# Cross-attention of layers 2 to 4 with the probabilities as stationary operand: 32x32 block transposes on VectorE and 32-row products in place of TensorE transposes

## The reference

```python
q = layernorm(x) @ Wq.T + bq             # 64 x 32 tokens, 16 heads of 16 features
k = ctx @ Wk.T + bk                      # 64 x 257 keys
v = ctx @ Wv.T + bv
scores = einsum('bhqd,bhkd->bhqk', q, k) / 4     # + mask or bias
attn = softmax(scores, axis=-1)
out = einsum('bhqk,bhkd->bhqd', attn, v)
x = x + out @ Wo.T + bo
```

## Time and profile before

| what | value |
|---|---|
| median of 3 runs | 3512.74 us |
| the profiled execution's own time, its span | 3512.3 us |
| PE busy in it | 3266.2 us, 93% |
| DVE, ACT, POOL busy | 63%, 41%, 29% |
| l1x, l2x, l3x together | about 1320 us, each about 440 us |
| steady stretch of l1x (14 tiles) | 379 us, PE busy 375.0 |

### The profile page before, as it was taken

One profiled execution on the slowest core, in us unless ns is written; L12 is line 12 of the kernel. 1 busy time (PEld: TensorE's weight loads), 2 busy tenths in 40 slices (PEclk: granted clock), 3 DMA queues, 4 the chain that ended last, 5 costly groups with the idle time before them and its releaser, 6 DMA issues. The chain is left out here.

```text
span 3512.3 us, 105565 instructions
## 1 busy us (share of the span) xinstructions
PE 3266.2 (93%) x39150; PEld 2585.9 (74%) x39150; DVE 2217.2 (63%) x7505; ACT 1454.0 (41%) x4212; POOL 1003.2 (29%) x1620
## 2 busy tenths in 40 slices
PE   7978999999987999999999999888999999988799
PEld 6767887777766888888877777765666777767576
DVE  4767226666667988889556666763334666668455
ACT  2334335555532333333255555541111555556222
POOL 0112113333243444444323333442110111112421
PEclk9989999999997999999999999979999999999699
DMA  6643332222112000000011111042112111110323
GB/s 222 212 177 154 115 100 58 57 57 54 62 40 103 3 2 2 2 2 2 13 44 45 43 43 44 2 146 98 46 46 69 43 39 39 39 35 2 114 79 113
DMA packets 145872, 225.26 MB, mean 64 GB/s; under 512 B 14216, under 2 KB 121480, under 8 KB 143816
## 3 DMA queue, kind: packets, MB, share of 16 engines
q1 hardware_dynamic: 138816, 203.16, 18.4%
q0 software_dynamic: 6816, 18.69, 1.5%
HBM read 201.03 MB, written 38.74 MB: 68 GB/s over the span
## 5 line engine op out<-in xcount | busy, mean ns | idle before, releaser
L3303 POOL TENSOR_TENSOR l1fu_second_weighed<-l1fu_second,l1fu_parts 128x256 bf16<-128x256 bf16 x384 | 273.0, 739 | 342.9 <-DVE l1fu_second L3544 336.0
L3355 PEld LDWEIGHTS l1fu_ps_u<-l1f_xnT_all,l1f_key_in 128*128 128x128 f32 x2048 | 252.5, 195 | 17.4 <-issue 11.2
L3355 PE MATMUL l1fu_ps_u<-l1f_xnT_all,l1f_key_in 128*128 (+1 forms) x2048 | 255.0, 279 | 8.7 <-issue 5.5
L3366 PE MATMUL l1fu_ps_y<-l1f_key_out,l1fu_units 128*128 128x256 f32 x1024 | 250.6, 389 | 1.7 <-DVE l1fu_units L3552 1.7
L3366 PEld LDWEIGHTS l1fu_ps_y<-l1f_key_out,l1fu_units 128*128 128x128 f32 x1024 | 185.7, 190 | 33.3 <-issue 6.0
L3417 ACT COPY l1fu_plane<-l1fu_ps_p 128x512 f32<-128x512 f32 x128 | 75.1, 586 | 249.4 <-PE l1fu_ps_p L3345 249.4
L3539 DVE TENSOR_TENSOR l1fu_first<-l1fu_index,l1fu_counted 128x1024 bf16<-128x1024 bf16 x128 | 165.0, 1289 | 20.3 <-PE l1fu_ps_p L3345 17.6
L3425 ACT ACTIVATE l1fu_units<-l1fu_ps_u 128x512 f32<-128x512 f32 x128 | 76.6, 599 | 150.6 <-PE l1fu_ps_y L3366 138.5
L3011 DVE TENSOR_TENSOR l2f_hidden<-l2f_hidden,l2f_ps_u 128x512 f32<-128x512 f32 x55 | 37.8, 688 | 148.9 <-PE l2f_ps_u L2755 139.1
L1020 ACT ACTIVATE l2x_scores<-l2x_scores,l2x_minus_big 128x257 f32<-128x257 f32 x256 | 129.2, 513 | 2.5 <-DVE l2x_minus_big L1104 2.4
L1020 ACT ACTIVATE l1x_scores<-l1x_scores,l1x_minus_big 128x257 f32<-128x257 f32 x256 | 129.2, 513 | 2.1 <-DVE l1x_minus_big L1104 2.1
(11 more groups left out here) (747 smaller groups left out, 8379.8 us busy)
## 6 DMA issues: line engine op xcount, KB each, us to landing
rows_by_expert<-in_zeros_dram SPq DMA_DIRECT2D x1, 17544.0 KB
l0x_ctxT<-in_ctx_T_dram SPq DMA_DIRECT2D x32, 514.0 KB, 5.2
l0x_ctx_rows<-in_ctx_dram SPq DMA_DIRECT2D x64, 256.0 KB, 3.4
l0f_w<-in_L_ffn_w_dram SPq DMA_DIRECT2D x16, 1024.0 KB, 5.1
l1x_ctx_sb<-in_ctx_T_dram SPq DMA_DIRECT2D x64, 256.0 KB, 2.8
l2x_ctx_sb<-in_ctx_T_dram SPq DMA_DIRECT2D x64, 256.0 KB, 2.8
l3x_ctx_sb<-in_ctx_T_dram SPq DMA_DIRECT2D x64, 256.0 KB, 2.8
l1x_mask_raw<-in_mask_int_dram SPq DMA_DIRECT2D x16, 514.0 KB, 3.9
```

What stands on the lines that cost most here:

```text
L3303: last = nc.gpsimd.tensor_tensor(second_weighed[:, k % 2, part], second[:, k % 2], parts[:, 1 - par, part, TC * k:TC * k + TC].unsqueeze(2 ...
L3355: last = nc.tensor.matmul(ps_u[:, k % 2, j, :], key_in[:, c, JS * k + j, :], xnT_all[:, c, bass.ts(tile, P)], start=(c == 0), stop=(c == C ...
L3366: last = nc.tensor.matmul(ps_y, units[:, k, j, :], key_out[:, JS * k + j, :], start=(k + j == 0), stop=(k == K - 1 and j == JS - 1))
```

## The change

Per batch, in each of the three cross-attentions:

- VectorE turns the probabilities within 32x32 blocks by one transpose of 128x1152 (9 blocks of 32 keys for each of 4 banks, the ninth filled up with zeros) in place of TensorE's 8 transposes, and of the copies out of PSUM on ScalarE and VectorE.
- `values` makes the values in the layout that this needs: 64 products of 128x32 by 64 columns, four beside each other in the array, in place of 4 of 128x128 by 256.
- `outputs` uses the turned probabilities [32 keys, 128] as the stationary operand: 36 products of 32 rows x 128 columns with 68 moving columns, four row groups beside each other, each row group into a bank of its own. The values carry a column of ones, which gives the sum; the last key is a ninth step with one row.
- `turn_shares`, `weigh`, `inverse`, `shares` are gone. ScalarE copies the values and (in four pieces of 32 partitions) the outputs; once per tile VectorE divides (`norm_context`), TensorE turns the tile (`turn_mixed`, two transposes) and ScalarE keeps it with the bias.
- keys and values have PSUM of their own; the outputs lie in the score banks, behind column 260.
- Start: GpSimd fills four tiles with zeros or ones, and four small DMAs spread the last key's values over partitions.

```diff
-            def turn_probs_1(at, before, draining):
-                for r in range(R):
-                    last = nc.tensor.transpose(ps_p[:, r, :], scores[:, b, r, 0:P], ident)
-            def turn_probs_2(at, before, draining):
-                for r in range(R):
-                    last = nc.tensor.transpose((ps_p2 if draining else ps_p)[:, r, :], scores[:, b, r, P:K2], ident)
...
+            def values(at, before, dst=ps_v):
+                for kb in range(KB):
+                    for c in range(C):
+                        for j in range(2 * HH):
+                            last = nc.tensor.matmul(dst[32 * j:32 * j + 32, kb, :], ctx_sb[:, b, c, 32 * kb:32 * kb + 32],
+                                                    by_group(c, j), start=(c == 0), stop=(c == C - 1),
+                                                    skip_group_check=True, tile_position=(0, 32 * j))
...
+            def outputs(at, before, ahead2):
+                if before:
+                    pe.wait_ge(per_batch["o_kept"][before[0]], before[1])
+                if ahead2:
+                    pe.wait_ge(per_batch["biased_ready"][ahead2[0]], ahead2[1])
+                pe.wait_ge(s["tail_values_put"], n)
+                pe.wait_ge(per_batch["v_kept"][b], n)
+                wait(pe, per_batch["probs_turned"][b], n)
+                for kb in range(KB + 1):
+                    for j in range(2 * HH):
+                        keys_of = slice(32 * j, 32 * j + (32 if kb < KB else 1))
+                        values_of = v[keys_of, b, kb] if kb < KB else v_last[keys_of, b]
+                        last = nc.tensor.matmul(ps_o[:, j, :], probsT[keys_of, b % 2, kb].rearrange("p r q -> p (r q)"),
+                                                values_of.rearrange("p r e -> p (r e)"), start=(kb == 0),
+                                                stop=(kb == KB), skip_group_check=True, tile_position=(32 * j, 0))
...
+                nc.vector.transpose(probsT[:, b % 2].rearrange("p k r q -> p r k q"),
+                                    scores[:, b].rearrange("p r (k q) -> p r k q", q=32)).then_inc(per_batch["probs_turned"][b], 1)
...
+            def fill():
+                nc.gpsimd.memset(v_tail[:], 0.0)
+                nc.gpsimd.memset(scores[:, :, :, KEYS:WIDE], 0.0)
```

More of the change, by code:

```diff
@@ L771, in turn @@
-            def turn(i, first, last):
-                n = i + 1
[L773 to L789, removed]
@@ L926, in tile_output, with turn @@
                 last.then_inc(s["y_ready"], 1)
-            def turn(i, first, last):
+            def turn(i, first, last, ahead_norm):
                 n = i + 1
@@ L1041, in turn @@
-            def turn(i, first, last):
+                act.wait_ge(per_batch["o_ready"][b], n)
+                if b == 0:
+                    after(act, s["ctx_normed"], n - 1)
+                for r in range(R):
+                    last = nc.scalar.copy(summed[32 * b:32 * b + 32, :, r],
+                                          ps_o[32 * r:32 * r + 32, :, HE * r:HE * r + HE].rearrange(
+                                              "p (c h) e -> p c h e", c=C))
+                last.then_inc(per_batch["o_kept"][b], 1)
@@ L1042, in turn, with keep_oT @@
+            def keep_oT(n):
+                act.wait_ge(s["mixed_turned"], n)
+                after(act, s["y_ready"], n - 1)
+                kept(oT[:], by_chunk(ps_mixed), "bv").then_inc(s["oT_kept"], 1)
+            def turn(i, first, last, ahead_norm):
                 n = i + 1
                 for t in range(BT):
-                    now, before2, ahead, ahead3 = (batch(t + k, n, first, last) for k in (0, -2, 1, 3))
-                    keep_probs(now, before2)
-                    if not last and t == 2:
+                    now, ahead, ahead3 = (batch(t + k, n, first, last) for k in (0, 1, 3))
+                    if ahead:
+                        exps(ahead, range(0, 2))
+                    if not last and t == 1:
@@ L1176, in turn @@
                     if ahead2:
                         maxima(ahead2)
[L1178 to L1187 removed]
+                    if not first and t == 0:
+                        norm_context(n - 1)
@@ new lines, in turn @@
+                    if not last and t == 1:
+                        spread_q(n + 1)
+                    if ahead_norm and t == 2:
+                        tile_stats(i + 2, n + 2)
+                    if not first and t == 2:
+                        add_output(i - 1, n - 1)
+                    if ahead:
+                        turn_probs(ahead, before)
+                    if ahead_norm and t == 3:
+                        tile_normed(i + 2, n + 2)
+            for i in range(2):
+                tile_stats(i, i + 1)
+                tile_normed(i, i + 1)
```

411 lines of the change are left out of this document (174 added, 237 removed).

## The result

The changed kernel takes 3968.54 us, median of 4 runs (3951.24 to 3981.26); the kernel before 3516.97 on the same chip (3510.6 to 3523.42). The ratio is 1.129, interval 1.1265 to 1.1318: 452 us slower, where 3596 had been predicted.

What follows compares the result with a forecast made beforehand. TensorE's stream was taken to set the pace. 15 steady tiles each at +1.36, +1.36 and +1.86 us gave +69; with ends +9 and starts +6, 3512.3 became 3596 us, range 3515 to 3760.

Steps and rivals of the forecast that it cites:

- sum per tile: TensorE's steady cross-attention tile: -7.76 + 9.20 + 0.22 + 0.20 = +1.86 us in l3x, +1.36 in l1x and l2x.
- Outputs: 36 products per batch in 18 waves of four row groups, 120 ns each and 0.14 first load: 2.30 us.
- Removed work: Both halves of the transposes, the shares and the old outputs go from TensorE: 7.76 us per tile.
- What both kernels do alike: Keys, scores, queries and output projection on TensorE were said to fall out of the difference.
- The new wait: Plain batch's outputs wait in the score banks until VectorE has read the scores of t+2: 0.2 us per tile.
- Hidden work: VectorE's block transpose, at most 1.60 us, and ScalarE's copies, about 0.22 each, stay hidden: about 15 and 18 of 28 us.
- the likeliest case: Whole kernel at 3596 us, its own range 3543 to 3643; chance 0.62.
- Ends: After each cross-attention's last values, 11.8 us to the last product in l2x, and 3 us more each: +9.
- Short loads: Rival: 32-row loads cost a fourth or hide fully, outputs 1.22 us, whole kernel 3402 us; chance 0.13.
- loads that take turns: Rival: one full-width load at a time for all row groups, outputs 8.13 us, whole 4646 us; chance 0.07.
- Waiting loads: Rival: a load waits for the product before it, wave 171 ns, or 162 by l3a's rate; whole 3733 us; chance 0.12.
- A wash: Rival: outputs at 105 ns a wave, no new wait, free ends: 3523 us at most; chance 0.06.

Runs made afterwards that it cites:

- the half columns: Changed kernel with half the values made in the loop; its outputs with 34 of 68 moving columns: 3540.95 us, or with 64 of 128 stationary columns: 3485.42 us.
- the kernel with all the work: Changed kernel, values of key blocks 0 to 2 made twice by an inner loop, blocks 5 to 7 left out: 3692.22 us, ratio 1.052.
- the written-out loop: Changed kernel with only TensorE's loop over tiles 1 to 13 written out in the three cross-attentions: 3736.9 us, ratio 1.065.
- the one at 3485 us: Changed kernel with half the values made in the loop, and key blocks 1 to 7 of the outputs with 64 of 128 stationary columns: 3485.42 us.
- six blocks: Changed kernel with key blocks 6 and 7 of the values left out in the loop's tiles: 3657.89 us.
- the four-tile kernel: Kernel before with TensorE's loop at four tiles per pass, 3 passes and two tiles written out: 3554.58 us, ratio 1.0126.

## Why the prediction was wrong

The direction was right, the size was not. The step that failed is the **sum per tile**: its terms were all prices of work, and "the time from one start to the next" was taken to be their sum. The change part by part counted 176 products becoming 458 only as time on the array. They are also text of a loop, and most or all of that text had to be fetched again in every pass: a term of 309 us that the sum has at nothing. The 442.7 us between the profiles' cross-attentions divide so:

| part | predicted, us | measured, us |
|---|---|---|
| 14 steady tiles x 3 at their prices (28.75 for a tile without stalls) | 64 | 76 |
| stalls and slow clock in the same tiles: 1516.1 - 42 x 28.75 | 0 | 309 |
| starts, first tile, ends | 20 | 58 |

Of the 309 us TensorE stands for 183.5; the other 125 are work at the lower clock behind the stalls.

The terms of work come out near the forecast in sum, and that is luck in part. *Values*: 1.92 predicted, 1.92 to 1.93 measured. *Outputs*: 2.30 predicted, 2.17 measured, 64 records (16 waves) in 1.81 to 1.84 us, 113 to 115 ns a wave instead of 120. The bound by the load was right, as the half columns show. An estimate by the rule of the Trainium skill in "TensorE: Matmul & The Clock Gate", section "LDWEIGHTS (loading the stationary operand)", is 107 ns a wave and 1.93 + 0.14 = 2.07 us, about as far below as the forecast was above. *turn_mixed*: 0.22 predicted, 0.31 measured.

*Removed work* was 7.4 us per tile and not 7.76. The plain batch that was read the earlier trace rows is the dearest of the four; in the others the old outputs take 0.58 or 0.59 instead of 0.70, and behind the queries the first half of the transposes takes 0.44. In the kernel before, and for the next reading two rows of the changed kernel:

```profile
772.76 0.65 PE L913 MATMUL l1x_ps_o<-l1x_probsT,l1x_v 128*32 128x64 f32 x32
773.35 0.66 PE L878 MATMUL l1x_ps_p<-const,l1x_scores 128*128 128x128 f32 x4
...
749.34 1.99 PE L850 MATMUL l1x_ps_k<-l1x_ctx_sb,weights 128*128 128x256 f32 x8
751.17 1.03 PE L917 MATMUL l1x_ps_x<-weights,l1x_oT 128*128 128x256 f32 x4
```

*What both kernels do alike* didn't fall out of the difference. Keys behind scores take 751.17 - 749.34 = 1.83 us, and as much ahead of turn_xn, where they took 1.73 behind the transposes; turn_xn takes 0.31 instead of 0.22, the output projection 0.96 instead of 0.86. The reason wasn't tried. *The new wait* for the maxima: a plain batch has 727.06 - 725.10 = 1.96 us from keys to outputs, 0.23 above 1.73, but 0.10 of that is in all keys that stand behind scores, and the wait is 0.13 where 0.2 was predicted. VectorE's last maximum ends at 726.96, the outputs start at 727.06:

```profile
725.10 1.99 PE L850 MATMUL l1x_ps_k<-l1x_ctx_sb,weights 128*128 128x256 f32 x8
727.06 1.33 PE L898 MATMUL l1x_ps_s<-l1x_v,l1x_probsT 32*128 32x68 f32 x37
...
726.88 0.08 DVE L1099 DVE_READ_ACCUMULATOR2_ANT l1x_big<- 128x1 f32 x1
```

Together, for l3x: -7.37 + 8.68 + 0.31 for removed work, outputs and turn_mixed, and 0.42 + 0.09 + 0.10 for keys with the wait, turn_xn and the projection, make +2.2 (26.54 to 28.75) where +1.86 was predicted. The outputs were priced 0.52 too high and the removed work 0.39 too high, and the rest stood at 0.42 where it measures 0.92.

*Hidden work* stayed hidden. The block transpose and the copies of the outputs:

```profile
703.95 1.37 DVE L1113 STREAM_TRANSPOSE l1x_probsT<-l1x_scores 128x1152 f32<-128x1152 f32 x1
...
707.16 0.87 ACT L1025 COPY l1x_summed<-l1x_ps_s 32x68 f32<-32x68 f32 x4 [1.32 <-PE l1x_ps_s L898]
```

1.37 us where at most 1.60 was said, four copies in 0.87 as said; in the kernel with all the work DVE is busy 48%, ACT 57% of the steady tiles. So the steady tile of 28.5 was off by 0.3, by errors that partly cancel, and the kernel with all the work and a pass that fits has 28.8. Its 3692 us less its branches (39 tiles x 1.14 us = 44) are 3648, just above the 3543 to 3643 of the likeliest case.

*Ends*: "I count 3 us more" was mis-sized. After the last values l1x needs 1068.44 - 1047.27 = 21.2 us to its last product (l2x 22.5, l3x 21.9), not 11.8 and 3:

```profile
1047.27 0.69 PE L879 MATMUL l1x_ps_s<-l1x_kT,l1x_q_by_half 32*64 32x257 f32 x16
1047.89 0.44 PE L908 MATMUL l1x_ps_t<-const,l1x_mixed 128*128 128x128 f32 x2
1049.85 2.02 PE L898 MATMUL l1x_ps_s<-l1x_v,l1x_probsT 32*128 32x68 f32 x64 [1.52 <-issue]
...
1053.80 2.05 PE L917 MATMUL l1x_ps_x<-weights,l1x_oT 128*128 128x256 f32 x4 [1.72 <-ACT l1x_oT L968]
1055.78 3.70 PE L898 MATMUL l1x_ps_s<-l1x_v,l1x_probsT 32*128 32x68 f32 x64
...
1060.97 3.70 PE L898 MATMUL l1x_ps_s<-l1x_v,l1x_probsT 32*128 32x68 f32 x64 [1.07 <-ACT l1x_summed L1025]
1066.97 0.66 PE L908 MATMUL l1x_ps_t<-const,l1x_mixed 128*128 128x128 f32 x2 [1.87 <-DVE l1x_mixed L1122]
1068.44 2.04 PE L917 MATMUL l1x_ps_x<-weights,l1x_oT 128*128 128x256 f32 x4 [0.81 <-ACT l1x_oT L968]
```

There is no next batch to fill the waits, and behind them the granted clock is 0.50 (from 1055.8 to 1059.5 us): the outputs take 3.7 us instead of 2.0. That is 30 of the 58 us, where 9 had been predicted for the ends. The first tile and the last two are written out and have the scattered stalls besides; what they make of the rest wasn't told apart. *Starts* were no matter: 10.0 to 12.5 us to the first turn of xn, before 10.5 to 11.0.

*The rivals.* Short loads and loads that take turns are refuted by the wave of 115 ns. Waiting loads would have been 171 ns a wave, and half the moving columns would have shortened it; their 3733 us stands beside the written-out loop's 3737 by chance. A wash wanted 105 ns a wave, no new wait and free ends, and had none of them. What happened was not among the rivals, though the trace of before had it: l1fu, a sublayer with a long loop, brings 80 instruction packets from 1120 to 1740 us while the cross-attention brings 5 in 380 us. The prediction named "a granted clock under 1.0 in steady tiles" as what would prove it wrong, and that is what came.

## What to carry to other kernels

A change that cuts products into smaller ones multiplies instructions, and in a loop their number has a bound of its own: count the instructions of one pass on the engine that sets the pace, before and after, and look at the instruction queue for a loop of this kernel that already fetches. A pass of 1300 fitted on TensorE, one of 1600 did so in some places, one of 1860 in none for good. Past the bound, writing the loop out is worth 6% here, but not enough: at 65 instructions per us even straight code lost 2 to 3 us per tile, and the change stays 6.5% slower than the kernel before. No version here that does the whole work beats the kernel before; the one at 3485 us leaves part of it out.

## What the runs showed of the hardware

- A branch back to instructions that aren't kept costs TensorE 3.0 to 5.3 us of standing, and behind it 2 to 8 us more per tile for work at half clock (from 1993.9 to 2037.0 us a tile of l2x takes 43.1 with a mean granted clock of 0.78). One that finds them costs 0.14 us (wide products around it) to 0.26 (narrow ones).
- A pass only a little too long can alternate. In l1x every second head of a tile stands for 4.5 to 5.1 us, the ones between for 0.2, and the passes bring 7 and 2 packets in turn; with six blocks l3x does the same. l1x brings 68 packets in 14 tiles where l2x brings 122; from 734 to 762 us, a tile's work without a stall, the instruction queue brings none.
- Four 32-row loads of 128 columns in different row groups do run beside each other, 115 ns for all four, where one alone comes every 111.
- TensorE's straight code with 1823 products and loads in a tile of 28.8 us is slowed by fetching, to 30.5 to 31.5 us; with 620 in 27.0 it isn't: the two tiles that the four-tile kernel has written out take 27.0 each in l1x and l2x.
